# A ring of four buffers for the gathered rows in a two-layer graph and expert network kernel on one core

## The reference, cut to what matters

```python
x = x + gnn0(layernorm(x))    # out = segment_sum(w_e * (ln @ Wl)[src_e], dst_e) + ln @ Wr + biases
x = x + ffn0(layernorm(x))    # 8 experts: y_e = relu(bn(relu(bn(ln@W1_e))@W2_e))@Wo_e, sum_e gate_e*y_e
x = x + gnn1(layernorm(x))    # the same gather, weigh and sum with the other sources and weights
x = x + ffn1(layernorm(x))    # one of 32 experts per row
```

## Time and profile before

| | |
|---|---|
| median of 3 runs | 2962.04 us (2961.93 to 2962.98) |
| the profiled execution | 2958.48 us, span 2956.5 us |
| mean granted TensorE clock | 0.945 of full speed |
| busy over the span | PE 88%, PEld 82%, DVE 73%, ACT 53%, POOL 66% |
| second stage's gathers | 784, mean 1251 ns, from 406.8 to 1677.3 us |
| second graph layer's gathers | 784, mean 1029 ns |

### The profile page before, as it was taken

How to read it: one execution, slowest core, us unless ns; L and a number is a source line. 1 busy time by engine, 2 the same in 40 slices (tenths; PEclk the granted TensorE clock), 3 DMA queues, 4 the chain that set the end, 5 groups by cost and what they waited for, 6 DMA issues and landing times. The chain is left out here.

```text
span 2956.5 us, 54481 instructions
## 1 busy us (share of the span) xinstructions
PE 2599.4 (88%) x19092; PEld 2420.7 (82%) x19092; DVE 2167.4 (73%) x5110; ACT 1565.7 (53%) x3295; POOL 1957.5 (66%) x1696
## 2 busy tenths in 40 slices
PE   5799935799999999999999994599999999999999
PEld 5799825788888888888888873489999999999999
DVE  8898836577787777777878754767777777777773
ACT  4477636788888888888888762111212112121212
POOL 0355557777777877777777501877777777777770
PEclk9999956799999999999999997689999999999999
DMA  2133454332333333233233203788888888888880
GB/s 74 6 82 77 93 137 144 91 97 78 109 108 91 99 108 110 79 107 110 78 115 108 80 1 114 212 205 214 204 215 214 212 208 215 213 213 209 212 212 24
DMA packets 241962, 390.31 MB, mean 132 GB/s; under 512 B 43642, under 2 KB 115218, under 8 KB 241426
## 3 DMA queue, kind: packets, MB, share of 16 engines
q0 software_dynamic: 163072, 310.24, 41.1%
q1 hardware_dynamic: 78324, 74.90, 8.0%
q10 hardware_dynamic: 288, 1.61, 0.1%
HBM read 343.43 MB, written 43.19 MB: 131 GB/s over the span
## 5 line engine op out<-in xcount | busy, mean ns | idle before, releaser
L1409 POOL DMA_INDIRECT f_got<-h_tab,list_cols x784 | 981.1, 1251 | 291.0 <-issue 219.1
L2121 POOL DMA_INDIRECT n_got<-h_tab,edge_cols x784 | 806.5, 1029 | 238.5 <-issue 227.6
L1690 DVE TENSOR_TENSOR f_hlo<-edge_cols,f_hhi 128x1024 fp32r<-128x1024 f32 (+1 forms) x208 | 242.0, 1163 | 294.3 <-ACT f_hhi L1498 294.1
L1585 PE MATMUL bank<-f_mhi,f_hot 128*128 128x256 f32 x1168 | 329.0, 311 | 131.2 <-DVE f_mlo L1684 131.1
L1468 ACT ACTIVATE f_got<-f_got,list_cols 128x256 f32<-128x256 f32 x784 | 333.9, 497 | 145.6 <-DMA f_got<-h_tab,list_cols 145.1
L2185 ACT ACTIVATE n_hrh<-bank 128x512 fp32r<-128x512 f32 x196 | 116.9, 597 | 535.6 <-PE bank L2254 535.6
L1585 PEld LDWEIGHTS bank<-f_mhi,f_hot 128*128 128x128 f32 x1168 | 247.6, 212 | 148.0 <-issue 143.8
L1493 ACT ACTIVATE edge_cols<-bank,f_shf,f_scl 128x512 f32<-128x512 f32 (+1 forms) x416 | 295.1, 743 | 106.9 <-PE bank L1400 76.7
L2232 PE MATMUL bank<-n_got,n_hot_h 128*128 128x256 f32 x784 | 242.2, 309 | 99.4 <-DMA n_got<-h_tab,edge_cols 59.0
L1586 PE MATMUL bank<-f_mlo,f_hot 128*128 128x256 f32 x1168 | 320.3, 304 | 0.0
L400 POOL DMA_INDIRECT list<-runs,off_i x98 | 158.0, 1612 | 215.2 <-DVE off_i L759 99.0
(11 more groups left out here) (331 smaller groups left out, 7833.0 us busy)
## 6 DMA issues: line engine op xcount, KB each, us to landing
f_got<-h_tab,list_cols POOLq DMA_INDIRECT x784
n_got<-h_tab,edge_cols POOLq DMA_INDIRECT x784, 3.8
n_rows<-acc_tab SPq DMA_DIRECT2D x24, 256.0 KB, 4.7
out_rows<-n_rows SPq DMA_DIRECT2D x24, 256.0 KB, 3.7
h_tab<-acc SPq DMA_DIRECT2D x37, 128.0 KB, 3.5
edge_cols<-in_w SPq DMA_DIRECT2D x16, 256.0 KB, 2.8
acc<-in_x SPq DMA_DIRECT2D x4, 896.0 KB, 7.9
h_tab<-hbuf SPq DMA_DIRECT2D x7, 512.0 KB
```

Of the source, the lines that this page charges most:

```text
L1409: nc.gpsimd.indirect_dma_start(got[:, s % RING0, u, :], None, h_tab[0], bass.IndirectOffsetOnAxis(gidx0[:, s * U + u:s * U + u + 1], 0), b ...
L1585: nc.tensor.matmul(tile_bank(t), lhs, mhi[:, s % 2, u, :], start=begins, stop=False)
L1690: nc.vector.tensor_tensor(hlo[l][:, :, 0:w], rl[:, :, 0:w], hhi[l][:, :, 0:w].bitcast(F32), ALU.subtract).then_inc(s_lo[l], 1)
L2121: nc.gpsimd.indirect_dma_start(got[:, s % RING, u, :], None, h_tab[1], bass.IndirectOffsetOnAxis(gidx[:, s * U + u:s * U + u + 1], 0), bou ...
```

## The change

The ring of gathered rows gets a fourth buffer, and with it a fourth `s_got` semaphore; POOL's wait before slot s is for `mlo` of slot s - 4 where it was for s - 3. The tensor `x4` (2 KB per partition) goes, and `got` grows by 4 KB per partition. The third staging buffer of the weights is now columns 256 to 511 of both halves of `xraw`.

```diff
-RING0 = 3
+RING0 = 4
...
-            x4 = sb3("x4", [P, F, 2 * P])
...
-            raw = [rl[:, :, 0:D], rl[:, :, D:2 * D], x4[:, :, :]]
+            raw = [rl[:, :, 0:D], rl[:, :, D:2 * D], xraw[:, :, D:2 * D]]
```

## The result

The changed kernel took 2932.49 us (median of 4 runs, 2924.23 to 2935.43) beside 2961.98 us (2958.32 to 2962.98) for the one before: a ratio of 0.9883, 95% interval 0.9864 to 0.9901, 29.5 us less. Forecast were 2930.0 us. The profiled execution is the fastest of the four, 2924.23 us, so its span is 34.2 us shorter than before's, where the medians differ by 29.5. Two later series of runs gave 0.989 (0.9873 to 0.9907) and 0.9895 (0.9868 to 0.9922).

A forecast was written before the change was run, and what follows sets the result against it. POOL, issuing gathers all the time from 600 us on with pauses forced by its buffers, was taken as the bound. -44 + 5 + 7 = -32 us gave 2926.5 us profiled, 2930.0 us as median; range 2903 to 2960 us.

The forecast's parts named there:

- The sum: Whole kernel: waits removed, rests kept and added stretching, -44 + 5 + 7 = -32 us against the profiled execution.
- The term of 0 until 600 us: Second stage until 600 us: POOL sets the pace alone, so a fourth buffer does nothing, 0 us.
- The staging at nothing: Weights' loads in the first slots: moving the third staging buffer costs nothing.
- The waits for the ring go: -44.0 us, 5 us of rests.: From 600 us: POOL's real waits for a free buffer, 44.0 us, go, except for an estimated 5 us.
- The gathers are stretched in the time given back: +7: From 600 us: VectorE stretches gathers in the 44 us given back too, at 0.154 us per us, +7 us.
- A: From 600 us, POOL without pauses sets the pace: 2915 to 2941 us, chance 0.63.
- PE's 77.2 us of waits left room: From 600 us: PE's 77.2 us of waits for `mlo` exceed the 32 us taken, so PE does not become the bound.
- B: No change: the consumers set the pace and POOL only waits earlier or later; 2956 to 2968 us, chance 0.14.
- C: More than the waits: mean gather falls to 1.19 us and PE becomes the bound; 2885 to 2910 us, chance 0.12.
- D: Slower: ring waits had kept POOL in step with VectorE; free-running, more gathers are stopped; 2982 us, chance 0.08.
- E: VectorE waits for gathers where POOL had paused, +39 us on -32: 2969 us, chance 0.03.
- What would show it: Signs from 600 us: POOL's real waits under 10 us, mean gather 1.24 to 1.28 us, ScalarE's and PE's waits 25 to 40 less.

The follow-up runs named there:

- thinned kernels: Changed kernel with three of four gathers a slot from the fifth on: 2901.83 us, ratio 0.9794; likewise with a ring of three: 2906.7 us, 0.9812.
- reordered kernel: Changed kernel with VectorE doing the next slot's lower messages before the second layer's lower half: 2950.71 us, ratio 0.9958 to the kernel before.
- staging-only kernel: Changed kernel with the ring back at three, so only the weights' third staging buffer moved: 3238.72 us on the slower chip, ratio 1.0007.
- thinned ring of three: Changed kernel with a ring of three and three of four gathers a slot from the fourth on: 3132.02 us (0.9694) on the slower chip, then 2906.7 (0.9812).

## Why the prediction was right, and where it was not

**The size.** 2930.0 us forecast, 2932.49 measured. The sum had -32 us for the profiled execution; the slots 32 to 192 gave -34.3.

**Where it acts.** The term of 0 until 600 us was nearly right: 4.8 us less from slot 0 to 32. They seem to belong to the earlier release, since the kernel with four buffers and the wait of three has 197.7 us there. The real waits for the ring from 400 to 600 us were 0.9 us before (4.8 us in 13 waits), so what the rest comes from stays open. Nearly all in the steady stretch: right. The staging at nothing: right, shown by two kernels.

**"The waits for the ring go: -44.0 us, 5 us of rests."** This step failed. 31.1 us of 44.0 stayed. What went were ScalarE's waits for rows, 76.8 to 0.3 us, about twice the most that I had asked for, and the round of the consumers closed in 102.0 us where 105.4 stood. That the rows are never late is what set it free is shown by the thinned kernels, whose ring waits are long and whose pace is the same.

**"The gathers are stretched in the time given back: +7."** It went the other way: the mean fell from 1263 to 1228 ns, 656 x 0.035 = -23 us. POOL's own account of its 656 gathers is then -13 (waits) - 23 (stretching) - 4 (gaps beyond 0.30 us) = -40 us, from 1079 to 1039 us. The slots 32 to 195 by `mlo` gained 33.3 us; the other 7 are POOL's greater lead over VectorE at the end, about one slot. The two errors, 26 us too much for the waits and 30 too little for the stretching, nearly cancelled. The kernel with four buffers and the wait of three shows the same exchange, 12 us of stretching against 14 of waits at one pace, so with the pace set by the consumers the two must fill what these take.

**Who sets the pace.** A said POOL. The thinned kernels say the consumers, at 102.0 us in 16 slots, POOL just under it. My sum for POOL without pauses was 1079 - 32 = 1047 us for 164 slots, or 102.1 us in 16. The two bounds lay that close together, so the time could not tell one from the other, and that it came out within 2.5 us is luck as far as the mechanism goes; the ring's waits and the thinned kernels tell them apart. I had written that PE's 77.2 us of waits left room; I had not asked how many of them were caused by gathers. The thinned kernel answers: 53 to 60 us of them were not.

**The rivals.** B named the right mechanism (the consumers' order, the 193.9 us before `hlo`), with the wrong pace: it took their pace as that of before, though ScalarE's 76.8 us stood in it. C's lower mean did not come, and its cap by PE was far too generous. D did not happen here. Its size was fair: a mean of 1.33 us was to use up the gain, and the reordered kernel with 1.326 us kept 12.6 us of 34.4, with some 8 us of its loss not due to gathers. E falls: VectorE's lower messages take 1217 ns where they took 1219, so a gather did not hold them up.

**What would show it.** ScalarE's waits: right in direction, more in size. PE's for `mlo`: -17.7 us where 25 to 40 were asked. Mean gather: 1228 ns, just under the range given. Last gather: 1634.6 where about 1645 was said, since a ring of four also lets POOL be a slot further ahead. POOL's real waits under 10 us: wrong with 31.1 us, and this is the row that tells the two bounds apart. I had also written that waits which stay at 40 us or more would mean that one slot more of lead was not enough. They stayed at 56.0 us, and it was enough: no row was late. What I had not allowed for is that a full ring can mean a POOL with time to spare.

## What to carry to other kernels

Here idle time on both sides of one ring, each for the other, meant that its depth cost time, and the further buffer paid back the part of the late side's waits that reached the pace (34 us, where ScalarE had 77 us of them). To know what sets the pace afterwards, thin one side: a quarter of the gathers taken away, with all waits between the other engines unchanged, settled it at once. And before an order on VectorE is changed, look whether gathers are issued beside it: a row of tensor-tensor instructions without a gap can stop one until its end.

## What the runs showed of the hardware that I had not expected

A gather can be held up through a whole chain of VectorE instructions: 4.50 us in place of 1.01 through six of them, where most stretched gathers wait for one. It ends 0.88 us after the last, as all that are stretched do (0.87 to 0.90 us in before's trace from 600 us on, for all 280 that took over 1.05 us). The Trainium skill's page SBUF — State Buffer, section "Who interferes with whom", has whichever of the two engines issues first keep the shared ports for its whole instruction, while the other blocks fully. Gathers that end behind the VectorE instruction they met agree with it. A gather held on through the next five is more than the rule says.

Which instructions follow each other matters. In the reordered kernel's trace from 600 us on 33 gathers took over 2.6 us, and 32 of these began while `mlo` ran with `hlo` straight behind it; seven more that met this pair got in between the two. All 97 that met `hot` with `mlo` straight behind it got in between. In the changed kernel's trace no gather met an `mlo` with an `hlo` straight behind it, and none took over 2.07 us. The order of the pair alone does not decide it: in before's trace nine gathers were held on from `hlo` through `mlo`, and 29 got in between these two. What does, no run here shows.

The chip of the second series ran all kernels, the one before too, 8 to 9% longer; the staging-only kernel had a granted TensorE clock of 0.911 over its span, where the kernel before had 0.945 on the first chip. Its second stage was lengthened less than the later ones: 109.7 us in 16 slots for 105.4, and 1492.8 us from the last `mlo` to the end for 1267.8. The kernels with a quarter fewer gathers took nearly the same there as on the first chip in this stage (102.6 beside 102.3 us for the ring of three). The ratio of the thinned ring of three was 0.9694 on it and 0.9812 on the other: an effect on one stage should not be carried from chip to chip as a ratio.
